# Local attention over the context in four groups instead of two, interleaved with the projections, with two steps moved from VectorE to ScalarE

## The reference, cut to what matters

```python
hid = jnp.tanh(jnp.einsum('btc,pc->btp', c_t, W_p))            # c_t = layernorm(x), P_SIZE = 100
p_t = Sq * jax.nn.sigmoid(jnp.einsum('btp,op->bto', hid, V_p)) # Sq = 77
win_low = p_t.astype(jnp.int32) - WINDOW_LENGTH                # WINDOW_LENGTH = 2
window = jnp.clip(win_low + jnp.arange(4), 0, Sq - 1)
scores = jnp.einsum('btwq,cq,btc->btw', qw, W_a, c_t)          # qw: the window's context rows
gauss = jnp.exp(-jnp.square(s_pos - p_t) / 2.0)
a_t = jax.nn.softmax(scores, axis=-1) * gauss
s_t = jnp.einsum('btw,btwq->btq', a_t, qw)                     # x = x + tanh(g) * s_t
```

## Time and profile before

| | us |
|---|---|
| median of 3 runs | 1552.63 |
| the runs | 1551.36 to 1558.65 |
| the profiled execution, its own time | 1555.33 |
| its span in the trace | 1553.0 |
| PE busy | 1219.1 (79%) |
| DVE busy | 933.2 (60%) |
| ACT busy | 502.3 (32%) |

### The profile page before, as it was taken

One profiled execution on the slowest core, in us unless ns is written; L12 is line 12 of the kernel. 1 busy time (PEld: TensorE's weight loads), 2 busy tenths in 40 slices (PEclk: granted clock), 3 DMA queues, 4 the chain that ended last, 5 costly groups with the idle time before them and its releaser, 6 DMA issues.

```text
span 1553.0 us, 22808 instructions
## 1 busy us (share of the span) xinstructions
PE 1219.1 (79%) x8642; PEld 913.3 (59%) x8642; DVE 933.2 (60%) x2369; ACT 502.3 (32%) x1118; POOL 195.1 (13%) x194
## 2 busy tenths in 40 slices
PE   4879899974798898966989798996999862899600
PEld 3657588863356545644656677883666561688500
DVE  5898812258547646973635653456899849455433
ACT  2444433331337553521515211321333320343200
POOL 0350000000000000002010000000000000555376
PEclk9999899985799999988999797996999955899855
DMA  9100000000000003000000800000111010455543
GB/s 348 51 1 2 1 1 0 0 1 0 0 1 2 1 1 109 1 1 21 1 21 1 229 1 1 0 1 0 34 34 34 2 55 3 130 162 158 116 130 117
DMA packets 57507, 68.81 MB, mean 44 GB/s; under 512 B 20869, under 2 KB 50431, under 8 KB 56639
## 3 DMA queue, kind: packets, MB, share of 16 engines
q1 hardware_dynamic: 49919, 46.98, 9.6%
q0 software_dynamic: 7488, 20.46, 5.2%
HBM read 50.62 MB, written 16.79 MB: 43 GB/s over the span
## 4 chain that ended last, share of the span: by engine, by line
PE 65%; DVE 19%; ACT 6%; POOL 4%; issue 4%; DMA 1%; another core or an unknown queue 0%; SPq 0%; DVEq 0%; POOLq 0%; ACTq 0%
PE ps L2334 5%; PE ps L1235 4%; PE ps L314 4%; POOL hall L2559 4%; PE ps L667 4%; PE ps L342 4%; PE ps L680 4%; PE ps L328 3%; PE ps L1740 3%; PE ps L2348 2%; PE ps L1754 2%; PE ps L354 2%; PE ps L1813 2%; PE ps L301 1%; ACT work L417 1%
## 5 line engine op out<-in xcount | busy, mean ns | idle before, releaser
L2548 POOL DMA_INDIRECT hall<-hall_rows,tile_idx x80 | 76.1, 951 | 488.6 <-DVE tile_idx L2474 436.3
L314 PE MATMUL ps<-hall,work 128*128 128x308 f32 x256 | 93.9, 473 | 19.7 <-DVE work L491 17.7
L2334 PE MATMUL ps<-big,work 128*128 x320 | 85.6, 391 | 3.4 <-ACT work L2386 3.4
L417 ACT COPY work<-ps 78x1024 f32<-78x1024 f32 (+1 forms) x64 | 64.3, 1005 | 70.6 <-PE ps L328 70.6
L1675 ACT ACTIVATE work<-ps,work 128x256 f32<-128x256 f32 x128 | 58.7, 472 | 84.8 <-DVE work L1566 84.7
L342 PE MATMUL ps<-work,hall 78*32 78x128 f32 (+1 forms) x2048 | 70.8, 280 | 8.7 <-DVE work L531 5.2
L328 PE MATMUL ps<-pack_const,work 128*78 128x128 f32 (+1 forms) x512 | 71.3, 284 | 0.0
L342 PEld LDWEIGHTS ps<-work,hall 78*32 78x32 f32 (+1 forms) x2048 | 53.3, 111 | 28.8 <-issue 14.4
L1235 PE MATMUL ps<-work,pack_F 128*128 128x256 f32 x288 | 66.4, 392 | 0.7 <-ACT work L1295 0.7
L2559 POOL DMA_INDIRECT hall<-expert_rows,back_idx x64 | 61.9, 968 | 38.9 <-DMA expert_rows<-work 19.7
L1740 PE MATMUL ps<-big,dpack 128*128 128x384 f32 (+1 forms) x160 | 64.4, 567 | 1.8 <-ACT big L1652 1.8
(11 more groups left out here) (483 smaller groups left out, 2760.3 us busy)
## 6 DMA issues: line engine op xcount, KB each, us to landing
expert_rows<-work SPq DMA_DIRECT2D x40, 256.0 KB
dpack<-in_fside SPq DMA_DIRECT2D x8, 616.0 KB, 4.9
dpack<-in_pack_D SPq DMA_DIRECT2D x1, 4115.0 KB, 18.4
hall_rows<-hall SPq DMA_DIRECT2D x2, 2048.0 KB, 10.5
big<-in_w SPq DMA_DIRECT2D x4, 1024.0 KB, 11.3
big<-in_pack_B SPq DMA_DIRECT2D x1, 2052.0 KB, 13.8
pack_F<-in_pack_F SPq DMA_DIRECT2D x1, 2052.0 KB, 24.6
x<-in_x SPq DMA_DIRECT2D x1, 2048.0 KB, 8.4
```

Of the source, the lines that this page charges most:

```text
L314: mm = nc.tensor.matmul(o, A["qT"][:, c, b * P:(b + 1) * P], KV["kbd"][:, c, b, k * 4 * SC:(k + 1) * 4 * SC], start=True, stop=L == "A")
L417: nc.scalar.copy(A["pT"][0:SK[L], u % 2, :].rearrange("p (k n) -> p k n", k=2), ps[0:SK[L], PT_BANK:PT_BANK + 2, :]).then_inc(s("pT_ready" ...
L2334: mm = nc.tensor.matmul(ps[:, GU_B[j % 2], 0:2 * INTER], MW["xT"][:, j % 2, c * P:(c + 1) * P], big[:, bass.ds(at + c * 2 * INTER, 2 * INT ...
L2548: gp.indirect_dma_start(out=FETCH_BUF[:, j % HT, :], out_offset=None, in_=hall_rows[:, :], in_offset=bass.IndirectOffsetOnAxis(ap=tile_idx ...
```

## The change

The stage works in four groups of two pairs (308 numbers wide) instead of two of four. `turn_a`, `take_aT`, `weigh` and `update` of a group are no longer behind all projections but in the loop over the pairs: on PE `turn_a` of group n/2 - 1 stands behind the projection of an even pair n (from 2 on), `weigh` behind that of the odd pair after it. DVE runs `counts` and `shifted` of a group after its odd pair and then `update` of the group before it; `weights` comes in the next even turn. ACT copies the scores out of PSUM in place of DVE, and squares the distances in place of DVE (in `gauss`, ahead of its exponential). `normed(n + 2)` waits for the turning of pair n on PE (`xT_ps`), no longer for the scores. The turned weights of every group go to one PSUM bank (6), and are copied to the two halves of `aT` in turn.

The diff, without the lines that only follow from the new size of the groups:

```diff
-    "a_ready": {"C": 2},
+    "a_ready": {"C": 4},
-        CG, CN = 2, HT // 2
+        CG, CN = HT // 2, 2
@@ local_pe
                 if n >= 2:
-                    pe.wait_ge(sem("C_score_taken"), n - 1)
                     pe.wait_ge(sem("C_ez_ready"), n - 1)
...
-            def turn_a(g, r):
+            def turn_a(g):
+                pe.wait_ge(sem("a_ready"), g + 1 + done("C", "a_ready"))
+                if g:
+                    pe.wait_ge(sem("aT_ready"), g + done("C", "aT_ready"))
...
-                    pe.wait_ge(sem("x_new"), 4 * (r + 1) + done("C", "x_new"))
+                    pe.wait_ge(sem("x_new"), 4 * g + done("C", "x_new"))
...
                 project_x(n)
-            for g in range(CG):
-                pe.wait_ge(sem("a_ready"), g + 1 + done("C", "a_ready"))
-                turn_a(g, 0)
-                turn_a(g, 1)
-                weigh(g, 0)
-                weigh(g, 1)
+                if n >= 2 and n % 2 == 0:
+                    turn_a(n // 2 - 1)
+                if n >= 3 and n % 2:
+                    weigh((n - 3) // 2)
+            turn_a(CG - 1)
+            weigh(CG - 1)
@@ local_act
-            def take_z(n):
-                act.wait_ge(sem("C_score_taken"), n + 1)
+            def take_score(n):
+                act.wait_ge(sem("s_ps"), n + 3 + done("C", "s_ps"))
+                nc.scalar.copy(CW["score"][:, n // CN, :, n % CN, :],
+                               ps[:, 3 + n % 2, 0:B * SC].rearrange("p (b s) -> p b s", b=B))
                 nc.scalar.activation(CW["ez"][:, n // CN, :, n % CN], ps[:, 3 + n % 2, B * SC:B * SC + B], ACT.Exp,
                                      scale=-1.0).then_inc(sem("C_ez_ready"), 1)
             def gauss(g):
                 act.wait_ge(sem("C_d2_ready"), g + 1)
+                nc.scalar.activation(CW["dist"][:, g], CW["dist"][:, g], ACT.Square).then_inc(sem("C_gauss_ready"), 1)
+                act.wait_ge(sem("C_gauss_ready"), 2 * g + 1)
                 nc.scalar.activation(CW["dist"][:, g], CW["dist"][:, g], ACT.Exp, scale=-0.5).then_inc(sem("C_gauss_ready"), 1)
...
                 take_hidden(n)
-                take_z(n)
-                if n == 4:
-                    gauss(0)
-                if n == 5:
-                    exps(0)
-            gauss(1)
-            take_aT(0, 0)
-            take_aT(0, 1)
-            exps(1)
-            take_aT(1, 0)
-            take_aT(1, 1)
+                take_score(n)
+                if n % 2:
+                    gauss(n // 2)
+                elif n:
+                    exps(n // 2 - 1)
+                if n >= 3 and n % 2:
+                    take_aT((n - 3) // 2)
+            exps(CG - 1)
+            take_aT(CG - 1)
@@ local_dve
-                ve.tensor_tensor(CW["dist"][:, g], CW["dist"][:, g], CW["dist"][:, g], ALU.mult).then_inc(sem("C_d2_ready"), 1)
...
             for n in range(HT):
-                if n == 6:
-                    weights(0)
-                take_score(n)
                 if n + 2 < HT:
+                    dve.wait_ge(sem("xT_ps"), n + 1 + done("C", "xT_ps"))
                     normed(n + 2)
-                if n == 3:
-                    counts(0)
-                if n == 4:
-                    shifted(0)
-            counts(1)
-            update(0, 0)
-            shifted(1)
-            update(0, 1)
-            weights(1)
-            update(1, 0)
-            update(1, 1)
+                if n % 2:
+                    counts(n // 2)
+                    shifted(n // 2)
+                    if n >= 3:
+                        update(n // 2 - 1)
+                elif n:
+                    weights(n // 2 - 1)
+            weights(CG - 1)
+            update(CG - 1)
```

More of the change, by code:

```diff
@@ L784, in project_x, with weigh @@
                 mm.then_inc(sem("s_ps"), 1)
-            def turn_a(g, r):
+            def turn_a(g):
+                pe.wait_ge(sem("a_ready"), g + 1 + done("C", "a_ready"))
+                if g:
+                    pe.wait_ge(sem("aT_ready"), g + done("C", "aT_ready"))
                 for k in range(4):
-                    mm = nc.tensor.transpose(ps[0:SC, (6, 2)[r], k * P:(k + 1) * P],
-                                             CW["dist"][:, g, (k % B) * CN + 2 * r + k // B, :], ident)
+                    mm = nc.tensor.transpose(ps[0:SC, 6, k * P:(k + 1) * P], CW["dist"][:, g, (k % B) * CN + k // B, :], ident)
                 mm.then_inc(sem("aT_ps"), 1)
-            def weigh(g, r):
-                pe.wait_ge(sem("aT_ready"), 2 * g + r + 1 + done("C", "aT_ready"))
+            def weigh(g):
+                pe.wait_ge(sem("aT_ready"), g + 1 + done("C", "aT_ready"))
                 if g:
-                    pe.wait_ge(sem("x_new"), 4 * (r + 1) + done("C", "x_new"))
+                    pe.wait_ge(sem("x_new"), 4 * g + done("C", "x_new"))
                 for k in range(4):
-                    nc.tensor.matmul(ps[:, ((5, 7), (0, 1))[r][k // B], k % B * D:(k % B + 1) * D],
-                                     CW["aT"][0:SC, r, k * P:(k + 1) * P], ctxN[:, k % B, :],
+                    nc.tensor.matmul(ps[:, (5, 7)[k // B], k % B * D:(k % B + 1) * D],
+                                     CW["aT"][0:SC, g % 2, k * P:(k + 1) * P], ctxN[:, k % B, :],
                                      start=True, stop=True).then_inc(sem("y_ps"), 1)
@@ L838, in exps, with take_aT @@
                 nc.scalar.activation(CW["e"][:, g], CW["e"][:, g], ACT.Exp).then_inc(sem("C_e_ready"), 1)
[L840 to L844, removed]
+            def take_aT(g):
+                act.wait_ge(sem("aT_ps"), g + 1 + done("C", "aT_ps"))
+                if g >= 2:
+                    act.wait_ge(sem("y_ps"), 4 * (g - 1) + done("C", "y_ps"))
+                nc.scalar.copy(CW["aT"][0:SC, g % 2, :], ps[0:SC, 6, :]).then_inc(sem("aT_ready"), 1)
             take_x(0)
@@ L875, in normed @@
                                      ALU.subtract, ALU.mult).then_inc(sem("xn_ready"), 1)
[L877 to L880, removed]
             def counts(g):
@@ L887, in counts @@
                 link(ve.tensor_scalar(pos[:, 1, :], pos[:, 0, :], float(SC), None, ALU.mult))
-                link(ve.tensor_tensor(CW["dist"][:, g], iota, over_s(pos[:, 1, :]), ALU.subtract))
-                ve.tensor_tensor(CW["dist"][:, g], CW["dist"][:, g], CW["dist"][:, g], ALU.mult).then_inc(sem("C_d2_ready"), 1)
+                ve.tensor_tensor(CW["dist"][:, g], iota, over_s(pos[:, 1, :]), ALU.subtract).then_inc(sem("C_d2_ready"), 1)
                 link(ve.tensor_scalar(pos[:, 2, :], pos[:, 1, :], MAGIC, None, ALU.add))
@@ L911, in weights, with update @@
                 link(ve.reciprocal(pos[:, 4, :], pos[:, 4, :]))
-                dve.wait_ge(sem("C_gauss_ready"), g + 1)
+                dve.wait_ge(sem("C_gauss_ready"), 2 * (g + 1))
                 link(ve.tensor_tensor(a, a, e, ALU.mult))
                 ve.tensor_tensor(a, a, over_s(pos[:, 4, :]), ALU.mult).then_inc(sem("a_ready"), 1)
-            def update(g, r):
+            def update(g):
                 for k in range(4):
-                    t = g * CN + 2 * r + k // B + k % B * HT
+                    t = g * CN + k // B + k % B * HT
                     if k % B == 0:
-                        dve.wait_ge(sem("y_ps"), (2 * g + r) * 4 + k + B + done("C", "y_ps"))
-                    finish(t, ps[:, ((5, 7), (0, 1))[r][k // B], k % B * D:(k % B + 1) * D], None, 1, None, sem("x_new"))
+                        dve.wait_ge(sem("y_ps"), g * 4 + k + B + done("C", "y_ps"))
+                    finish(t, ps[:, (5, 7)[k // B], k % B * D:(k % B + 1) * D], None, 1, None, sem("x_new"))
             normed(0)
```

## The result

The changed kernel took 1566.98 us, median of 9 runs (1562.03 to 1569.01), the kernel before 1557.37 us in as many (1551.36 to 1559.78): ratio 1.0068, 95% interval 1.0051 to 1.0084. It is slower by about 10 us. Forecast were 11.2 us and 1563.8; the kernel before itself had moved, from the 1552.6 of its first three runs to 1557.4 in nine.

What follows compares the result with a forecast made beforehand. Bound: a DVE-PE chain, per pair before, per group after. Full-clock stage end 380.5 + 0.6 x 16.1 = 390.2, 11.2 us later than 379.0; 1552.63 + 11.2 = 1563.8 us, range 1554.5 to 1570.5.

Steps and rivals of the forecast that it cites:

- The tie: On PE turn_a(g) precedes odd pair 2g + 3, which DVE's counts(g + 1) needs: three DVE waits, 3.4 to 6 us each.
- The second wait: At half clock DVE's weights waits for ACT's exps, behind PE's weigh and the even pair: 3.2 us, in two rounds.
- half clock all the way: Rival: PE at 1.2 GHz throughout the new stage, +17.6 us, 1570.2 us; chance 0.17.
- DVE's work: counts, shifted and weights cost 7.5 us per group, four times; less score copies moved away, DVE gets 4.7 us more work.
- 12.4 less 9.3: At half clock, from the start of counts: ACT's exps path takes 12.4 us, DVE stands at weights after 9.3.
- the rival at full clock: Rival: PE at 2.4 GHz throughout the new stage, +1.5 us, 1554.1 us; chance 0.12.
- The clock: PE's clock falls ahead of turn_a(0), then is mixed: six tenths of 16.1 us is added to the full-clock end, 380.5.
- The start: Scores of pair 0 ready at 318.6, pair 1 follows without gap, and counts(0) on DVE begins at 321.9.
- The total: Stage ends at 390.2, 11.2 us later than 379.0; whole kernel 1563.8 us against the median 1552.63.
- what follows the stage is the same work: The program behind the stage was taken to move by the same amount as the stage's end, 11.2 us.

Runs made afterwards that it cites:

- Taking the tie away: Changed kernel with turn_a(g) on PE moved behind the projection of odd pair 2g + 3, directly ahead of weigh(g): ratio to before 1.0003, 1546.99 us.
- the experiment on `exps`: Changed kernel with exps(g) on ACT moved to the head of even turn 2g + 2, ahead of take_x, take_hidden and take_score: ratio to before 1.0055, 1553.90 us.
- the later comparisons: Follow-up timings on three chips; the changed kernel, unaltered, against the kernel before again: ratios 1.0115 and 1.0108, 1563.09 and 1562.97 us.

## Why the prediction was right

**The tie** (`turn_a` ahead of the odd pair, `counts` behind it) was the right step. Forecast were waits of 3.4 to 6 us ahead of `counts`; the last three were 4.4, 5.7 and 5.7. Taking the tie away gave back as much as the change had lost.

**The second wait**, 3.2 us twice at half clock, was 1.5 and 2.8. Its price, for half clock all the way, was a little high, its worth too low, as the experiment on `exps` showed.

**DVE's work.** 308-wide instructions were put at 0.48, 0.32 and, on ACT, 0.45; the rows show:

```profile
L894 DVE TENSOR_TENSOR work<-work 128x308 f32<-128x308 f32 x4 | 1.9, 480 | 0.1
...
L830 ACT COPY work<-ps 128x154 f32<-128x154 f32 x8 | 2.3, 288 | 8.8 <-PE ps L781 8.8
...
L837 ACT ACTIVATE work<-work 128x308 f32<-128x308 f32 x4 | 1.8, 459 | 4.7 <-DVE work L886 4.7
...
L898 DVE TENSOR_SCALAR work<-work 128x308 f32<-128x308 f32 x4 | 1.3, 320 | 0.1
```

`counts`, `shifted` and `weights` of a group came to 3.2, 1.9 and 2.2 us, 7.3 where 7.5 were forecast, so DVE got 3.9 us more work by the same sum, not 4.7. Two slips of the reckoning change nothing: 12.4 less 9.3 is 3.1, not 3.2, and the lower end of the range, 1554.5, lies above the rival at full clock, 1554.1.

**The clock.** At six tenths between full and half, the time from `turn_a(0)` to the end should have been 60.2 us (380.5 less 330.0, plus 0.6 x 16.1); it was 61.3, which is 0.67 of the way. The choice of that share was the weakest number, and it held partly by luck: counted in time, PE was at half clock for nearly eight tenths of these 61 us (mean 0.61), not six. That this cost no more than 0.67 of the way may be because PE's clock costs nothing while DVE is the engine that is waited for; that was not tested. From 369 on the clock stayed at half, 24 us with 13.9 us of matmuls; why it did not rise there as in the rounds before was not tested.

**The start** was not foreseen: the clock fell at 314, ahead of the first turning, where it had held before, and `counts(0)` came 10.6 us behind the stage's start where 9.4 had been reckoned. The change is not the cause: PE waits 3.28 us ahead of its first matmuls of the stage (L753) in every trace, and they took 2.4 us in a later trace of the kernel before as well, but 1.32 in the first one and in the second trace of the changed kernel. That and the share of the clock make up the 2.1 us by which the stage moved more than the forecast (13.3 instead of 11.2).

**The total** is right in sign and size in the first comparison (9.6 us between the medians, 11.9 between the spans), but with luck: the stage moved by 2.1 us more than forecast, and the part behind it was 2.1 us shorter than before. In the later comparisons the difference was 17.5 us both times, near the upper end of the range (17.9), and in their traces the part behind the stage was 3 to 4 us longer than before. The forecast took for granted that "what follows the stage is the same work" and moves by the same amount. The work is the same, its time is not.

**The mistake in the change**, seen from here: it joins a good part (the moves to ACT, 0.9962 alone) to one that costs more than twice what that gains (the regrouping, 1.0088 and 1.0098 alone), as it makes PE's stream wait for DVE in front of the work that DVE needs next.

## What to carry to other kernels

In streams written by hand, ask of each waiting instruction what stands behind it on its engine, and whether the engine that is waited for will need that next; if so, interleaving makes the two engines take turns. Move such an instruction behind the independent work; here that one move was worth 12.5 us of the stage. Where PE waits in each round, price its work at half clock first, and read the overlap off the trace of the slow engine. And test the parts of a joint change alone: here one gains 6 us by itself, which the time of the whole change does not show.

## What the runs showed of the hardware that was not expected

The same instructions outside the stage took different times from trace to trace. The stage began at 307.5 to 314.1 us in the traces of kernels that are alike up to there, and the part behind the stage took 1161.7 to 1167.8 us in the later comparisons (1170.4 and 1172.5 in the first): 0.4% of the program, as much as some of the effects tested. The later traces of one kernel agree within 1 us (1167.4 and 1166.6 for the changed kernel, 1161.7 and 1161.9 for the regrouping alone), so it may in part be an effect of what stands ahead; two traces each can't tell. In that part DVE was busy for 706.5 to 707.6 us in all fourteen traces, PE for 902.1 to 908.3, by and large more where the part was longer. That points to PE's clock as what differs, but was not tested.

The same stillness of PE ahead of the same matmuls did not always take the clock down. Behind the 3.28 us ahead of L753 they ran at full clock in some traces and at half clock in others, of the kernel before and of the changed one alike. With it the start of `counts(0)` moved, by 0.8 us between two traces of the changed kernel and by 1.6 between the two kernels with two groups and both moves.

In the three kernels with two groups and one or both moves to ACT, the layer norm behind the stage took 16.9 to 17.4 us instead of 15.5 in all others, with DVE's pairs of normalisations 1.55 to 1.61 us apart instead of 1.41 and nothing waited for. The instructions are the same. This takes back 1.4 to 1.9 us of what the stage gained; the cause stays open.
